# Four places for the counts of a group of nodes, and a bank readied once in two counting steps

## The reference

```
edge_index = stack([src, dst])
x = layernorm(x + mlp_mean(x, edge_index, edge_attr))       # an edge MLP, the mean per target, a node MLP
x = layernorm(x + two_attention_convs(x, edge_index))       # softmax over the edges of each target, twice
x = layernorm(x + three_sage_convs(x, src, dst))            # h @ Ws + mean over edges(h[src]) @ Wn + b, relu
x = layernorm(x + softmax_aggregation(x, edge_attr, src, dst))
```

## Time and profile before

| | |
|---|---|
| median of 3 runs | 3344.82 us (3343.13 to 3345.17) |
| the profiled execution | 3345.75 us, its span 3343.9 us |
| busy: TensorE products / weight loads | 2435.4 us (73%) / 1945.3 us (58%) |
| busy: VectorE / ScalarE / GpSimd | 2224.2 us (67%) / 1651.9 us (49%) / 1591.8 us (48%) |
| granted TensorE clock, mean over the span | 0.754 |
| readying products (L1012) | 784, 154.2 us busy, 197 ns each |
| readings of counts (L1424) | 784, 261.7 us busy, 334 ns each |

### The profile page before, as it was taken

The page is one execution under the profiler, slowest core; times in us unless marked ns, Lnnn a source line. Parts: engine busy times, 40 slices in busy tenths (PEclk is TensorE's granted clock), DMA queues, the critical chain, the costliest instruction groups (busy, mean ns, idle before and its releaser), DMA issues.

```text
span 3343.9 us, 48124 instructions
## 1 busy us (share of the span) xinstructions
PE 2435.4 (73%) x11311; PEld 1945.3 (58%) x11311; DVE 2224.2 (67%) x5084; ACT 1651.9 (49%) x3627; POOL 1591.8 (48%) x1656
## 2 busy tenths in 40 slices
PE   6777777846767676447767765999988966666675
PEld 4665665525555555335555554888877865555563
DVE  5888888456666666636666667444778676666668
ACT  2887887615555555345555553442222444444443
POOL 4777772067777650177777730000000017777770
PEclk8999999965555555555555556999999988888887
DMA  6555552035544441244444424675778754444440
GB/s 207 156 160 155 160 161 85 4 86 112 113 106 111 106 105 45 60 105 110 106 107 108 111 51 143 233 242 188 240 249 262 252 193 145 151 151 149 152 142 21
DMA packets 390935, 463.38 MB, mean 139 GB/s; under 512 B 168359, under 2 KB 290366, under 8 KB 385712
## 3 DMA queue, kind: packets, MB, share of 16 engines
q1 hardware_dynamic: 324758, 262.57, 26.8%
q0 software_dynamic: 63088, 192.63, 21.1%
q10 hardware_dynamic: 2828, 5.18, 0.5%
HBM read 383.76 MB, written 76.37 MB: 138 GB/s over the span
## 4 chain that ended last, share of the span: by engine, by line
PE 44%; DVE 21%; POOL 14%; issue 11%; ACT 3%; DMA 3%; DVEq 2%; ACTq 1%; SPq 0%; POOLq 0%
POOL y_and_h L745 12%; PE ps L1000 12%; PE ps L1067 11%; PE ps L877 6%; PE ps L1016 5%; DVE y_and_h L1693 3%; DVE big L1665 3%; PE ps L964 3%; DVE ps L1685 2%; DVE ps L2175 2%; DVE ea_sb L2181 2%; POOL big L731 2%; DMA maxima_blocks<-ea_sb 2%; ACT w_sb L1424 2%; PE ps L813 1%
## 5 line engine op out<-in xcount | busy, mean ns | idle before, releaser
L731 POOL DMA_INDIRECT big<-table_gat,src_idx x832 | 805.6, 968 | 629.1 <-DMA table_gat<-y_and_h 309.8
L1665 DVE TENSOR_TENSOR big<-big,ps 128x257 f32 (+3 forms) x1664 | 593.1, 356 | 297.7 <-PE ps L1000 69.1
L1424 ACT ACTIVATE w_sb<-ps 128x200 uint16 x784 | 261.7, 334 | 567.8 <-PE ps L1016 560.2
L745 POOL DMA_INDIRECT y_and_h<-table_pool,src_block x391 | 394.8, 1010 | 169.9 <-issue 118.9
L716 POOL DMA_INDIRECT big<-table_mlp,src_block x391 | 371.5, 950 | 157.6 <-issue 116.7
L1471 ACT ACTIVATE big<-big 128x3432 f32<-128x3432 uint16 (+1 forms) x72 | 210.1, 2919 | 367.6 <-PE ps L1067 367.6
L760 POOL DMA_DIRECT2D big<-adj x36 | 19.2, 532 | 712.9 <-ACT big L1471 643.9
L877 PE MATMUL ps<-w_sb,ea_sb 128*128 128x256 f32 x832 | 210.7, 397 | 128.8 <-DVE y_and_h L1693 117.3
L1067 PE MATMUL ps<-big,y_and_h 128*128 128x264 f32 (+1 forms) x1200 | 276.3, 392 | 22.9 <-DVE w_run L2218 22.8
L1223 PE MATMUL ps<-big,y_and_h 128*128 x624 | 195.7, 468 | 132.4 <-DVE big L2283 130.7
L1000 PE MATMUL ps<-y_and_h,rows 128*128 128x136 f32 (+1 forms) x672 | 191.9, 444 | 112.1 <-DVE big L1665 111.7
(11 more groups left out here) (350 smaller groups left out, 5340.0 us busy)
## 6 DMA issues: line engine op xcount, KB each, us to landing
big<-adj POOLq DMA_DIRECT2D x33, 1650.0 KB, 8.6
rows<-in_ea_swept SPq DMA_DIRECT2D x194, 256.0 KB, 3.5
adj<-w_sb SPq DMA_DIRECT2D x784, 50.0 KB
ea_sb<-in_ea_blocks SPq DMA_DIRECT2D x416, 64.0 KB
ea_sb<-rel_rows SPq DMA_DIRECT2D x208, 128.0 KB
maxima_blocks<-ea_sb SPq DMA_DIRECT2D x97, 256.0 KB, 2.6
rows<-in_ea_rows SPq DMA_DIRECT2D x97, 256.0 KB, 2.6
s_run<-border_flat SPq DMA_DIRECT2D x146, 128.2 KB, 5.9
```

Source lines behind the costliest of these rows:

```text
L731: pool.indirect_dma_start(ring[:, step % GAT_RING, :], None, table[k], bass.IndirectOffsetOnAxis(src_idx[:, step:step + 1], 0))\
L745: pool.indirect_dma_start(pool_rows[q][:, i, :], None, table["pool"], bass.IndirectOffsetOnAxis(src_block[:, block:block + 1], 0)).then_in ...
L1424: act.activation(staging[:, (4 * quad + j) % STAGED, :], ps[:, 6:8, :][:, bass.ds(halves_of[j + 1], 1), 0:CW].rearrange("p o n -> p (o n)" ...
L1665: dve.tensor_tensor(to, to, bank_of(j), ALU.add).then_inc(accumulated, 1)
```

## The change

A group of nodes now has one of four places for its counts, two in each of the two banks: its number modulo 4, times 256 columns in the two banks joined (`count_banks`). Two groups in a row that share a bank lie in different halves of it. Two counting steps can reach at most the next two groups, and the places of those are free. A bank is readied only ahead of steps 0 and 2 of a quad, and it is the bank opposite to that of the step before. Its column (200 or 712) stands in a table of its own. So the table `bank_tab`, which takes the place of `half_tab` and lies in `xT`, free at that time, has three numbers for two steps: the column that readies, and two places. TensorE and ScalarE load six numbers of it per quad in place of five. `lay_steps` works the table out with more operations on one row of 784 numbers.

```diff
--- before.py
+++ after.py
@@ -302,7 +302,7 @@
         past = w_sb[:, 0:NCH * HALF_A].bitcast(BF16).rearrange("p (c s) -> p c s", c=NCH)
         src_i, lo_i = w_sb[:, 0:STEPS_A].bitcast(I32), w_sb[:, STEPS_A:2 * STEPS_A].bitcast(I32)
         lo_tab, col_tab = extra[:, 0:HALF_A].bitcast(BF16), extra[:, HALF_A:2 * HALF_A].bitcast(BF16)
-        half_tab = extra[0:1, 784:784 + STEPS_A + 4].bitcast(I32)
+        bank_tab = xT[0:1, 0:STEPS_A // 2 * 3].bitcast(I32)
         addr_tab = extra[0:1, 1576:1576 + STEPS_A].bitcast(I32)
         step_tmp = extra[:, 2360:2360 + STEPS_A]
         ones_b = y_words[:, 1808:1808 + P // 2].bitcast(BF16)
@@ -529,17 +529,19 @@
             first, lo_quad, hi_quad = QUADS_FROM[k]
             return lo_quad + q - first if first <= q < first + hi_quad - lo_quad else None
 
-        def step_halves(eng_type, quad, n):
+        def step_sums(eng_type, quad):
 
             return nc.values_load_multi_w_load_instructions(
-                half_tab[0:1, quad * 4:quad * 4 + n], engines=(eng_type,), min_val=0, max_val=1,
-                skip_runtime_bounds_check_because="the parity of a group of nodes, counted on the chip")[1]
+                bank_tab[0:1, quad * 6:quad * 6 + 6], engines=(eng_type,), min_val=0, max_val=3 * 256,
+                skip_runtime_bounds_check_because="one of four places for a group's counts, or the column that readies a bank")[1]
 
         def step_places(eng_type, quad):
 
             return nc.values_load_multi_w_load_instructions(
                 addr_tab[0:1, quad * 4:quad * 4 + 4], engines=(eng_type,), min_val=0, max_val=SUBS_IN_DRAM - 1,
                 skip_runtime_bounds_check_because="groups of nodes and spare places, counted on the chip")[1]
+
+        count_banks = ps[:, 6:8, :].rearrange("p a n -> p (a n)")
 
         base = {k: NG * n for n, k in enumerate(PASSES)}
 
@@ -1002,18 +1004,19 @@
                     if pair:
                         mm.then_inc(summed, 1)
 
-                def count_step(quad, j, halves_of):
+                def count_step(quad, j, sums_of):
 
                     if quad is None:
                         return
                     step = 4 * quad + j
                     if j == 0:
                         pe.wait_ge(quad_ready, quad + 1)
-                    pe.matmul(ps[:, 6:8, :][:, ::-1, :][:, bass.ds(halves_of[j], 1), CW:CW + 1].rearrange("p o n -> p (o n)"),
-                              zero_block[:, 0:P], zero_block[:, 0:1], start=True, stop=True, skip_group_check=True)
+                    if j % 2 == 0:
+                        pe.matmul(count_banks[:, bass.ds(sums_of[3 * (j // 2)], 1)], zero_block[:, 0:P], zero_block[:, 0:1],
+                                  start=True, stop=True, skip_group_check=True)
                     if step:
                         pe.wait_ge(step_read, step)
-                    pe.matmul(ps[:, 6:8, :][:, bass.ds(halves_of[j + 1], 1), 0:CW].rearrange("p o n -> p (o n)"),
+                    pe.matmul(count_banks[:, bass.ds(sums_of[j + j // 2 + 1], CW)],
                               lo4[quad % QUAD_BUFS][:, :, j], col4[quad % QUAD_BUFS][:, :, j], start=False, stop=True,
                               skip_group_check=True).then_inc(step_counted, 1)
 
@@ -1024,20 +1027,20 @@
                     quad = quad_at(k, q)
                     if quad == 0:
                         pe.wait_ge(steps_ready, 1)
-                    halves_of = None if quad is None else step_halves(mybir.EngineType.PE, quad, 5)
-                    count_step(quad, 0, halves_of)
+                    sums_of = None if quad is None else step_sums(mybir.EngineType.PE, quad)
+                    count_step(quad, 0, sums_of)
                     if q < NG:
                         add_terms(q)
-                    count_step(quad, 1, halves_of)
+                    count_step(quad, 1, sums_of)
                     for later, stage in stages.items():
                         if q >= later and (q - later) % BATCH == 0 and (q - later) // BATCH < NK:
                             stage((q - later) // BATCH)
                     if q >= WEIGH:
                         sum_weighted(q - WEIGH, 0)
-                    count_step(quad, 2, halves_of)
+                    count_step(quad, 2, sums_of)
                     if q >= WEIGH:
                         sum_weighted(q - WEIGH, 1)
-                    count_step(quad, 3, halves_of)
+                    count_step(quad, 3, sums_of)
 
             pe.wait_ge(read_by["act"], fills_read(FIRST_FILL["gT"], "act"))
             attention_pass("gat1")
@@ -1412,7 +1415,7 @@
                     quad = quad_at(k, q)
                     if quad == 0:
                         act.wait_ge(steps_ready, 1)
-                    halves_of = None if quad is None else step_halves(mybir.EngineType.Activation, quad, 5)
+                    sums_of = None if quad is None else step_sums(mybir.EngineType.Activation, quad)
 
                     def read_step(j):
 
@@ -1422,8 +1425,7 @@
                             act.wait_ge(adj_stored[quad % (STAGED // 4)], 64 * (quad // (STAGED // 4)))
                         act.wait_ge(step_counted, 4 * quad + j + 1)
                         act.activation(staging[:, (4 * quad + j) % STAGED, :],
-                                       ps[:, 6:8, :][:, bass.ds(halves_of[j + 1], 1), 0:CW].rearrange("p o n -> p (o n)"),
-                                       ACT.Copy).then_inc(step_read, 1)
+                                       count_banks[:, bass.ds(sums_of[j + j // 2 + 1], CW)], ACT.Copy).then_inc(step_read, 1)
 
                     if MARK <= q < NG + MARK:
                         mark_nodes_of(k, q - MARK, read_step)
@@ -1851,8 +1853,15 @@
                 dve.drain().then_inc(steps_laid, 1)
                 row_i, spare_row = src_i[0:1, :], w_sb[0:1, n:2 * n]
                 link(dve.tensor_copy(row_i, sub_f[0:1, :]))
-                dve.memset(half_tab[:, 0:1], 1)
-                link(dve.tensor_scalar(half_tab[:, 1:n + 1], row_i, 1, None, ALU.bitwise_and))
+                link(dve.tensor_scalar(row_i, row_i, 3, None, ALU.bitwise_and))
+                link(dve.tensor_copy(place_row, row_i))
+                link(dve.tensor_scalar(spare_row, place_row, 2.0, -2.0 * 256, ALU.is_ge, ALU.mult))
+                link(dve.tensor_scalar(spare_row, spare_row, float(2 * 256 + CW), None, ALU.add))
+                link(dve.tensor_scalar(place_row, place_row, 256.0, None, ALU.mult))
+                pairs = bank_tab[:, :].rearrange("o (m k) -> o m k", k=3)
+                dve.tensor_copy(pairs[:, :, 1:3], place_row.rearrange("o (m k) -> o m k", k=2))
+                dve.tensor_copy(pairs[:, 1:, 0:1], spare_row.rearrange("o (m k) -> o m k", k=2)[:, 0:n // 2 - 1, 1:2])
+                link(dve.memset(pairs[:, 0:1, 0:1], CW))
                 link(dve.tensor_copy(row_i, step_no[0:1, :]))
                 link(dve.tensor_scalar(row_i, row_i, STAGED - 1, None, ALU.bitwise_and))
                 link(dve.tensor_copy(spare_row, row_i))
```

## The result

| | median us | ratio to before (95%) |
|---|---|---|
| before, run beside it | 3344.99 | |
| after the change | 3385.86 (3382.23 to 3390.08, 4 runs) | 1.0116 [1.0104, 1.0129] |

The change makes the kernel 41 us slower; 3325 was forecast. The profiled execution took 3382.23 us. The readying products are down to 392 as intended, and yet the attention passes are longer.

A forecast was written before the change was run, and what follows sets the result against it. No engine being full, the order of work, handed between TensorE and ScalarE, was taken to bound it. 3345.75 - 23.6 (readying) + 3 (other chains) + 1.1 (set-up) = 3326.2, against the median 3325.3; said 3325 us, range 3314 to 3339.

The forecast's parts named there:

- the price of the added register: Sixth number in each group's register load on TensorE and ScalarE: taken as 0, upper bound another 250 ns.
- rival (c): Six-number load, off its old four-word pitch, takes two more accesses, 500 ns, ahead of readying 0: 3370 us; chance 0.06.
- (a): Sixth register costs another 250 ns on TensorE, delaying count 0; 0.05 or 0.08 us lost per group: 3334 us; chance 0.12.
- the cover there: TensorE slack ahead of count 0, hiding a longer load: 0.24 us, second pass 0.21, less the 0.07 gained.
- ScalarE's cover: ScalarE's load lies under the one-hot's last operation; 0.25 us more would just be covered.
- The readying: Two of four readying products removed in each of 196 groups: 23.6 us gained, less 3 for other chains.
- Step 1: Readying ahead of count 1 removed: 0.10 us gained in each of 122 groups, 12.2 us.
- Step 3: Readying ahead of count 3 removed: 0.07 us gained and carried on, in 163 groups, 11.4 us.
- The address: Each counting product and read still computes one address from one register, now a column: put at 0.
- The set-up: Added VectorE table operations ahead of the first count: +1.1 us left on the path, between 0.5 and 2.
- Rival (b): VectorE takes over in all groups but the plain ones, leaving about 10 us of gain: 3335 us; chance 0.10.
- The gather (d): GpSimd's gathers, 42.91 us apart per batch, take over and nothing is left: 3345 us; chance 0.06, with other covers.

The follow-up runs named there:

- the run with TensorE's load mended: The changed kernel with TensorE alone loading eight numbers from a second table of pitch eight, ScalarE keeping the change's table: 3368.75 us, ratio 1.0088.
- eight-number kernel: The changed kernel with eight words of table per quad and all eight loaded, two of them unused: 3326.49 us, ratio 0.9944.
- four-number kernel: The changed kernel loading only the four places per quad, the readying column taken from the previous place's register by a reversed view: 3324.45 us, ratio 0.9938.
- the kernel with every readying: The four-number kernel with a readying product ahead of every step again, two more per quad: 3335.74 us, ratio 0.9981.

## Why the prediction was wrong

**The step that failed** is the price of the added register: "That looks like a second access begun by the fifth number, which the sixth would share. I take 0", with an upper bound of "another 250 ns". Measured: 240 ns in every second quad and 930 in the others (0.83 and 1.52 against 0.59). The bound was drawn from two rows, four and five numbers, both of tables whose pitch of 16 bytes kept every load on a multiple of 16; the change's pitch of 24 bytes did not, and the sum never asked what the address does. The row of 577 to 587 ns, quoted against rival (c) as "no sign of places that cost more", held no load from another kind of place, and so could not show one. The lower bound, "since more numbers can't load faster", is wrong too: eight load in 0.59 us where six take 0.82.

**The place and the sequence were right.** Readying 0 and count 0 are where the load comes to light, as (a) and (c) had it, and the cover there was some 0.2 us. With the prediction's own arithmetic and the measured loads, the short ones lose 0.05 to 0.08 us, as in (a), the long ones, 0.68 us above (a), 0.73 to 0.76; over 71 groups of each that is 71 x (0.065 + 0.75) = 58 us on 3325: 3383. Measured: 3385.86. That the sum comes so near is in part luck: beside the trace of the kernel that loads eight numbers, in rounds 11 to 99, the 84 groups with a long load lose 62 us from count 0 to count 0, 0.74 each, and the 83 with a short one win 9 back. Rival (c) had this mechanism, at 500 ns in all groups, and 3370, with a chance of 0.06; its price was too low, and it was thought too unlikely.

**ScalarE's cover** was put at 0.25 us, just enough. That held for the loads of 0.76; for those of 1.4 it is gone, and the run with TensorE's load mended shows what it costs: 1.0088 against 0.9944, some 48 us (42 by the medians).

**The readying.** 23.6 us less 3 were forecast; some 14 were measured. Step 1, at 12.2, came to 8 or 11, by the order in which they are removed. Step 3, at 11.4 ("0.07 is gained ... carried on"), came to 3 or 7: of the 0.07 that the count wins at its start, 0.04 are lost before its read. A plain group wins 0.10 us in the first pass and 0.12 in the second in place of 0.17 and 0.19. That is a term mis-sized, not a wrong mechanism.

**The address** was put at 0, with a thought only for a dearer one. It is cheaper, 46 ns in place of 55, and that is worth 8 us (0.9977). That the eight-number kernel lands at 3326, so close to the forecast, comes from these two errors, some 7 us and 8, which nearly cancel: luck in part.

**The set-up**: 1.1 us forecast, 1.1 measured (13.60 against 12.50 from the copy ahead).

**Other chains kept part of the gain.** In the four-number kernel the plain group takes 4.42 us (901.42 to 905.84 is one), where 4.40 was forecast; but of the 0.15 gained some 0.05 are the cheaper address's (4.57 before, 4.51 with it and every readying, medians of the first pass).

```profile
901.42 0.35 PE L1026 MATMUL ps<-big,y_and_h 128*128 128x200 bf16 x1 [0.39 <-ACT w_sb L1437]
```

Rival (b) had something of it. From the kernel with every readying to the one with two per quad, count 0 to count 0 in rounds 11 to 99, 63 plain groups win 7.1 us together and 43 groups at the batch stages 6.6, but the 61 groups in rounds that leave 1, 2 or 7 when divided by eight win nothing. In the stretch of 745 to 1300 us TensorE's weighted sums wait longer for VectorE's accumulation, first with every readying, then with two:

```profile
PE ps L1008 <- DVE big L1677: 96.2, 40, 4.4
```

```profile
PE ps L1008 <- DVE big L1677: 103.6, 45, 4.5
```

(The columns are us in total, times and the longest.) That speaks for VectorE, but no run shows that it is what holds those groups. A batch of the second pass comes to 45.63 us in the four-number kernel, in place of 46.45 and of the 45 that eight groups at 0.17 would give. The gather (d) did not stand in the way of all of the gain.

```profile
1619.55 0.21 DVE L1951 TENSOR_TENSOR y_and_h<-big,y_and_h 128x32 f32<-128x32 f32 x1
...
1665.18 0.21 DVE L1951 TENSOR_TENSOR y_and_h<-big,y_and_h 128x32 f32<-128x32 f32 x1
```

## What to carry to other kernels

A table of numbers that sequencers load was priced well here by accesses, not by numbers: lay each load on a multiple of 16 bytes in groups of four, and fill up to a multiple of four (eight took 0.59 us) rather than load two loose ones (six took 0.82). When a change alters a table's pitch, ask what it does to the addresses; a row of the old kernel says nothing about an alignment that the old kernel never used. Where two engines load the same numbers side by side, mending one shows little until the other is mended too.

## What the runs showed of the hardware

- TensorE's register load: 0.33 us for four numbers on a multiple of 16 bytes, 0.59 for five, 0.82 for six, 0.59 for eight; 1.24 for five and 1.52 for six from 8 bytes off. ScalarE's are 0.02 to 0.1 us shorter.
- The Trainium skill, "Runtime: NRT & Kernel Launch", section on instruction fetch mechanics, has some 200 ns per register even in bulk. The loads from 8 bytes off come near that, with 0.25 per number (1.24 / 5, 1.52 / 6); the aligned fours at 0.33 don't. "DMA: Bandwidth & Descriptors" of the Trainium skill, section on latency and other measured facts, gives a `tensor_load` a floor of some 600 ns; the trace calls these loads TENSOR_LOAD, and the shortest kind takes 0.33 us. Where the page and the trace differ, the trace decides.
- An address operation from a register that counts columns takes 46 ns (60 in the view that runs backwards), one from a register that counts banks 55.
- A count that follows the weighted sums directly starts 0.07 us sooner than behind a readying product of one column, but its result is read only some 0.03 us sooner.
